# Graph rows on GpSimd, interleaved scatters and a shorter routing in the mixing part of a graph-transformer layer

## What is computed

```python
xn = layernorm(x)                                   # 6250 x 256
x = x + gnn(xn, src, dst) + mix(xn)                 # graph part and mixing part
x = x + ffn(layernorm(x))                           # two of six experts per row

# mix: k, v = instance_norm of heads of xn @ w_kv; dots = k^T v; out = (q dots / N) @ w_out + b_out
# ffn:
rh = relu(features @ router_w1 + router_b1)
expert_logits = softmax(rh @ router_w2 + router_b2)
top_w, top_i = top_k(expert_logits, 2)
routing_weights = softmax(top_w)
out = sum over the two chosen experts of routing_weight * expert(features)
```

## Time and profile before

| | us |
|---|---|
| median of 3 runs | 760.2 (759.32 to 762.78) |
| the profiled execution | 756.72 |
| its span | 754.7 |
| mixing part, first mix product to last `row_ready` | 274.3 to 413.7 |
| experts' first input transfer | from 426.8 |
| TensorE busy, share of the span | 89% |
| VectorE, ScalarE, GpSimd busy | 74%, 58%, 59% |

### The profile page before, as it was taken

One profiled execution on the slowest core, in us unless ns is written; L12 is line 12 of the kernel. 1 busy time (PEld: TensorE's weight loads), 2 busy tenths in 40 slices (PEclk: granted clock), 3 DMA queues, 4 the chain that ended last, 5 costly groups with the idle time before them and its releaser, 6 DMA issues.

```text
span 754.7 us, 15722 instructions
## 1 busy us (share of the span) xinstructions
PE 673.2 (89%) x4705; PEld 621.3 (82%) x4705; DVE 555.3 (74%) x1423; ACT 441.1 (58%) x878; POOL 448.4 (59%) x392
## 2 busy tenths in 40 slices
PE   3878999999999979889885099999999999999993
PEld 2868888888888868777764089999999999999993
DVE  5665569998888876877786357777777777777773
ACT  2546567667776636767763145665665665656651
POOL 3547388877666500325556468888888865455555
PEclk9989999999999999988995579999999999999997
DMA  8785644444444268588734478666546965654443
GB/s 223 164 191 139 162 129 127 125 127 122 128 131 129 62 211 290 170 256 249 222 99 139 130 211 191 122 126 121 113 84 100 173 114 95 98 88 58 50 44 37
DMA packets 90673, 104.68 MB, mean 139 GB/s; under 512 B 27196, under 2 KB 74746, under 8 KB 90594
## 3 DMA queue, kind: packets, MB, share of 16 engines
q1 hardware_dynamic: 58049, 70.98, 33.4%
q0 software_dynamic: 32544, 32.70, 25.0%
HBM read 53.25 MB, written 52.26 MB: 140 GB/s over the span
## 4 chain that ended last, share of the span: by engine, by line
PE 77%; DVE 10%; DMA 3%; ACT 3%; POOL 2%; issue 2%; SPq 1%; POOLq 0%; DVEq 0%; ACTq 0%
PE kv_ps L1357 10%; PE kv_ps L1358 10%; PE kv_ps L1359 10%; PE pt L1349 6%; PE d_ps L1221 6%; PE kv_ps L1198 5%; PE kv_ps L1201 5%; PE kv_ps L1199 5%; PE xt_ps L1349 3%; PE kv_ps L1298 2%; PE pt L1201 2%; PE pt L1198 2%; PE pt L1199 2%; POOL tab L588 1%; PE pt L1289 1%
## 5 line engine op out<-in xcount | busy, mean ns | idle before, releaser
L1357 PE MATMUL kv_ps<-we_h,now_h 128*128 x648 | 193.6, 299 | 3.7 <-DVE now_l L1168 2.2
L1358 PE MATMUL kv_ps<-we_l,now_h 128*128 x648 | 184.4, 285 | 0.0
L1359 PE MATMUL kv_ps<-we_h,now_l 128*128 x648 | 184.3, 284 | 0.0
L1357 PEld LDWEIGHTS kv_ps<-we_h,now_h 128*128 128x128 f32 x648 | 125.1, 193 | 5.2 <-issue 5.2
L1358 PEld LDWEIGHTS kv_ps<-we_l,now_h 128*128 128x128 f32 x648 | 125.4, 194 | 0.0
L1359 PEld LDWEIGHTS kv_ps<-we_h,now_l 128*128 128x128 f32 x648 | 124.9, 193 | 0.0
L1148 DVE TENSOR_TENSOR work<-kv_ps,be 128x256 f32<-128x256 f32 x216 | 81.7, 420 | 52.8 <-PE kv_ps L1359 52.6
L610 POOL DMA_INDIRECT out_x<-work,arena x56 | 87.6, 1564 | 41.9 <-DVE work L1156 26.0
L788 ACT ACTIVATE now_h<-pt 128x512 fp32r<-128x512 f32 x54 | 32.5, 602 | 105.9 <-PE pt L1349 105.9
L556 POOL DMA_INDIRECT alg<-al_tab,src_all x50 | 62.3, 1245 | 39.2 <-issue 25.2
L960 DVE TENSOR_REDUCE ss<-xring 125x16 f32<-125x1040 f32 x50 | 61.7, 1234 | 16.9 <-ACT xring L673 15.9
(11 more groups left out here) (249 smaller groups left out, 1836.1 us busy)
## 6 DMA issues: line engine op xcount, KB each, us to landing
arena<-tab SPq DMA_DIRECT2D x80, 131.0 KB, 2.9
xring<-in_x SPq DMA_DIRECT2D x26, 224.0 KB
xt_tab<-arena SPq DMA_DIRECT2D x10, 568.8 KB
we_h<-wt_h SPq DMA_DIRECT2D x6, 768.0 KB, 6.0
we_l<-wt_l SPq DMA_DIRECT2D x6, 768.0 KB, 8.8
weight_in<-tab SPq DMA_DIRECT2D x28, 131.0 KB, 2.6
xring<-in_x SPq DMA_DIRECT2D x5, 560.0 KB
out_x<-arena SPq DMA_DIRECT2D x12, 224.0 KB
```

The lines of the kernel that those rows point to most:

```text
L1357: pe.matmul(outp, hi[:, c, :], we_h[:, w], start=c == 0, stop=False)
L1358: pe.matmul(outp, hi[:, c, :], we_l[:, w], start=False, stop=False)
L1359: last = pe.matmul(outp, lo[:, c, :], we_h[:, w], start=False, stop=c == KC - 1)
```

## The change

- `graph_rows` moves from VectorE to GpSimd. It is one add of 125 x 512 instead of two of 125 x 256, in place: it writes into the input buffer, and `y2` is gone. `mixed_rows` reads the input buffer. GpSimd does the first three pairs ahead (`EARLY`) and then pair i+3 in its step i.
- There are seven input buffers instead of five; the two new ones lie where `y2` was. They are loaded after the experts' biases. A buffer is loaded again when `mixed_rows` has read it (`x2_done`), no longer when the graph add has (`y2_done`).
- The scatters of a group are issued two per GpSimd step, from step `ENDS[g] + 4`, each two followed by one graph add.
- Routing has 25 operations per group instead of 28 (18 linked), in three parts. The first choice is made from the logits before the exp, so it needs no division and stands in part 0 with step A; step B holds ten operations instead of sixteen; step C is as before.
- SyncE reads the start addresses of the first expert tile before it waits for the scatters.

```diff
-SLOTS = 5
+SLOTS = 7
+EARLY = 3
-AL_STEPS, R_STEPS = 6, 21
-ROUTE_STEPS = (0, 1, 9, 15)
+AL_STEPS, R_STEPS = 6, 18
+ROUTE_STEPS = (0, 4, 12)
@@ SyncE @@
-            for i in range(SLOTS):
+            for i in range(SLOTS - 2):
                 load_x2(i)
...
             for b in range(2):
                 sp.wait_ge(cv_out[b], 16 * ROUNDS)
+            for i in range(SLOTS - 2, SLOTS):
+                load_x2(i)
             for i in range(PR):
                 if i + SLOTS < PR:
-                    sp.wait_ge(y2_done, i + 1)
+                    sp.wait_ge(x2_done, i + 1)
                     load_x2(i + SLOTS)
...
             sp.wait_ge(fill_out[0], 16 * (E + 1))
+            early = [sp.value_load(tab_row[0:1, 0, h:h + 1], min_val=0, max_val=E * REG) for h in range(HB)]
             for g in range(GROUPS - RB, GROUPS):
                 sp.wait_ge(sc_out[g % RB], scattered(g))
@@ GpSimd @@
-            for g in range(GROUPS):
-                pool.wait_ge(row_ready, g + 1)
-                for j in range(2 * SIZES[g]):
-                    pool.indirect_dma_start(out=tab0, ...).then_inc(sc_out[g % RB], 16)
+            def graph_rows(i):
+                pool.wait_ge(x2_in[i % SLOTS], 32 * (i // SLOTS + 1))
+                rows = x2in[i % SLOTS].rearrange("p l (h n) -> p l h n", n=GC)
+                pool.tensor_tensor(rows, rows, gsum[:, 2 * i:2 * i + 2, :].unsqueeze(2).to_broadcast([P, 2, GH, GC]),
+                                   ALU.add).then_inc(y2_done, 1)
+            pool.wait_ge(gs_done, CHUNKS)
+            for i in range(EARLY):
+                graph_rows(i)
+            for i in range(PR + 8):
+                for g in range(GROUPS):
+                    for j in range(2 * SIZES[g]):
+                        if ENDS[g] + 4 + j // 2 == i:
+                            scatter(g, j)
+                if i + EARLY < PR:
+                    graph_rows(i + EARLY)
@@ VectorE @@
-            graph_rows(0)
...
-                dve.tensor_tensor(xr[g % RB][:, at:at + 2, 0:D], ma_ps[i % 2][0:P, :, :], y2[i % 2],
+                dve.tensor_tensor(xr[g % RB][:, at:at + 2, 0:D], ma_ps[i % 2][0:P, :, :], x2in[i % SLOTS],
                                   ALU.add).then_inc(x2_done, 1)
...
+                def first(k):
+                    link(dve.reduce_max(tws[6], lg0, axis=AX.X))
+                    return dve.tensor_tensor(oh[:, k, :, 0:m]..., lg0, bc(tws[6], EP), ALU.is_equal)
                 if part == 0:
                     dve.wait_ge(lg_done, 2 * ENDS[b])
                     link(dve.reduce_max(tws[0], lgp, axis=AX.X))
                     dve.tensor_tensor(lg1, lgp, bc(tws[0], EP), ALU.subtract).then_inc(lgx_ready, 1)
                     dve.tensor_copy(row[:, :, C_TOK].bitcast(I32), ...)
+                    dve.wait_ge(lgx_ready, b + 1)
+                    link(dve.scalar_tensor_tensor(lg0, lg1, 0.0, order, ALU.is_ge, ALU.mult))
+                    link(first(0))
                 elif part == 1:
                     dve.wait_ge(ex2_done, b + 1)
                     link(dve.reduce_sum(tws[1], lg2, axis=AX.X))
+                    link(dve.scalar_tensor_tensor(lg3, oh[:, 0]..., -4.0, lg2, ALU.mult, ALU.add))
                     link(dve.reciprocal(tws[1], tws[1]))
-                    link(dve.tensor_tensor(lg3, lg2, bc(tws[1], EP), ALU.mult))
-                    link(choose(0, lg3))
-                elif part == 2:
-                    link(dve.scalar_tensor_tensor(lg2, oh[:, 0]..., -4.0, lg3, ALU.mult, ALU.add))
-                    link(choose(1, lg2))
-                    dve.tensor_tensor(tws[4], tws[3], tws[2], ALU.subtract).then_inc(d_ready, 1)
+                    link(dve.reduce_max(tws[3], lg3, axis=AX.X))
+                    dve.scalar_tensor_tensor(tws[4], tws[3], -1.0, tws[1], ALU.add, ALU.mult).then_inc(d_ready, 1)
+                    link(dve.tensor_tensor(lg1, lg3, bc(tws[3], EP), ALU.is_equal))
+                    link(dve.tensor_tensor(lg0, lg1, order, ALU.mult))
+                    link(first(1))
                     dve.tensor_tensor_scan(cum..., carry..., oh..., 0.0, ALU.mult, ALU.add).then_inc(oh_ready, 1)
@@ loop of VectorE @@
-                if i + 1 < PR:
-                    graph_rows(i + 1)
-                for part, lag in ((3, 4), (1, 3), (2, 3), (0, 2)):
+                for part, lag in ((2, 4), (1, 3), (0, 2)):
```

43 lines of the change are left out of this document (15 added, 28 removed).

## The result

The changed kernel takes 766.2 us (763.56 to 767.05, five runs) against 760.88 us (759.32 to 762.78) for the kernel before, run beside it: ratio 1.0084, 95% interval [1.0061, 1.0107]. It is slower, by 4.6 to 8.1 us. I had predicted 756.7 us and a range up to 762.0 us. The profiled execution is one of 766.52 us, its span 764.6 us.

The account below looks back on a forecast made before the run. It took the mixing part's chain to alternate between TensorE and, in steps B and C, VectorE with ScalarE. 1.3 + 2.3 + 1.2 = 4.8 us, less 1.3 us held, gave 3.5 us: 760.2 to 756.7 us, range 751.0 to 762.0.

Parts of the forecast that it names:

- Start of the mixing part: Before the first product and first transposes: without VectorE's graph adds there, both come earlier, a gain of 1.3 us.
- Steps B and C: Routing steps: VectorE loses work, but ScalarE can give back only its waits for VectorE; a gain of 2.3 us.
- End: Between landed scatters and the first expert tile: SyncE's start addresses are read ahead, taking 1.2 us from the path.
- GpSimd, nothing on the path: Mixing loop: two scatters and a 1.1 us add make 4.1 us against a mean step of 5.1 us, costing nothing.
- The held operations: Mixing part: GpSimd's adds hold VectorE operations with two SBUF inputs; 0.25 us per group, 1.3 us lost, ends 0 and 5.5.
- The slack: VectorE, before step C's square root: slack of 0.4 us and more, said to speak against costly holds.
- slower by the held operations: Steps A to C: two held operations per group on the path, 11 us against 4.8 us gained; 766 us, chance 0.10.
- ScalarE takes all: Steps B and C give nothing, leaving start and end, 2.5 us, less some of it; 758.5 us, chance 0.25.
- GpSimd as the bound: Mixing loop: an add over 2.1 us would make GpSimd's step exceed the loop's 5.1 us; about 762 us, chance 0.03.
- the clock rival: Mixing loop: shorter TensorE idle times in step C may keep its clock up, some 5 us; 751.7 us, chance 0.17.

Follow-up runs that it names:

- f2: The changed kernel with the graph adds back on VectorE at their old place, two of 125x256; 752.73 us, ratio 0.9943 to the kernel before.
- f1: f2 with one 125 x 512 graph add per pair on VectorE, behind mix_l and in step A; 751.41 us, ratio 0.9909 to the kernel before.
- f3: The changed kernel run once more; 764.44 us, ratio 1.0078 to the kernel before.
- e1: The same kernel as f2, run on a chip with disturbed experts; 784.24 us, ratio 1.000 to the kernel before.
- e3: The changed kernel with a one-column GpSimd write and a wait before each graph add from pair 4 on; 785.03 us, ratio 0.999.
- h4: f1 with one spare-tile write on VectorE in step B of each group, ahead of line 1050's place; 764.75 us, ratio 1.0046 to the kernel before.
- g3: f1 with three chained spare-tile writes on VectorE in step B of each group; 796.01 us, ratio 1.0154 to the kernel before.
- g2: f1 with twenty extra TensorE products in step 24 and early reads ahead of the fill-up wait; 777.82 us, ratio 0.9937 to the kernel before.

## Why the prediction was wrong

**Start of the mixing part, 1.3 us.** The size was right: the first transposes come 8.6 us after G before and 8.7 in f2, 7.3 in f1. In the change they come at 8.3, and 1.0 of the gain is lost again (f3 24.4, f1 23.4 at the same clock). GpSimd does ten adds in a row there, since no scatters stand between them yet, and the sixth (282.40) runs beside line 1050 of pair 0, which takes 1.12 us instead of 0.16; ScalarE's rows and the first transposes stand behind it. I had costed the removal at this place and the holds only "in steps A to C".

The start in the changed kernel:

```profile
276.18 2.51 POOL L593 TENSOR_TENSOR xring<-xring,gsum_sb 125x512 f32<-125x512 f32 x2 [16.03 <-DVE gsum_sb L967]
...
277.05 0.39 PE L1281 MATMUL kv_ps<-bo_hl,sel_hl 128*128 128x256 f32 x1 [0.93 <-DVE wg_l L1019]
...
282.56 1.12 DVE L1050 SCALAR_TENSOR_TENSOR work<-mv,work 125x2 f32<-125x2 f32 x1
...
283.72 1.09 ACT L757 ACTIVATE staged<-work 125x256 f32<-125x256 f32 x2 [0.91 <-DVE work L1050]
```

The product starts 0.95 us after G instead of 1.57: 0.6 us earlier, where I had forecast 0.7.

**Steps B and C, 2.3 us.** Right. The way from the logits to the square root of step C is 0.5, 0.7, 0.5, 0.5 and 0.3 us shorter in f1 than before, 2.6 us in all; in f2 and e1, which keep the adds in step B, it is 2.5 and 2.8 us. That square root has no idle time before it in cycles that are not held, and the one of step B comes 0.3 us later, where I had 0.4 to 0.5.

**End, 1.2 us.** Right: R5 to the first tile is 20.6 us before, 19.3 after, 18.8 in f2, where the transfer starts 0.9 us after the last landing instead of 2.1 (I had said 0.1 to 0.3). What I missed is that the early reads stand behind the wait for the fill-up transfers, which in the change end last. The chain of waits there:

```profile
429.92 5.37 DMA tab<-skip_rows
...
435.37 0.28 SPq L482
...
436.00 0.27 SPq L482
...
437.55 2.05 DMA arena<-tab
```

**GpSimd, nothing on the path.** Right as far as waits go: the adds take 1.27 to 1.29 us where I took 1.1 and 1.29 as the upper bound, no mixed rows wait for one, and a step of GpSimd is 4.2 us (352.24 to 356.42) against 4.7 us and more of the loop.

**The held operations, 0.25 us per group.** This is the step that failed: 1.3 us in all were forecast, and moving the adds costs 11.7 us (f2 against f3). The mechanism was right and read from the right row; its price was too small by about a factor of ten in the three cycles from A1 to A4, where it delays the square root of step C by 3.2, 2.8 and 2.4 us, and it was nothing in groups 0 and 4. To these 8.5 us come 1.0 us at the start and the clock. Four things made it so:

- The length. I capped a hold at one add, "up to its own length". It begins with the scatter in front of the add, and two adds in a row make one hold: 2.7 us at 329.08. e3 shows this part.
- The number. I took a share of time in which VectorE is critical, a quarter to a third, as if the adds fell at random. They don't: `row_ready` starts the scatters and so fixes the adds against the steps A to C behind it. Both traces of the change have their long holds at the same few lines, 1050, 1068, 1082 and 1089.
- The slack. I set 0.4 us and more of slack before step C against the holds. It is there, 0.9 us, and takes up its part of each hold behind line 1050. But lines 1068 and 1050 stand ahead of it, where h4 shows none (0.57 to 0.59 us per cycle for a delay of as much), and a hold of 1.7 or 1.9 us behind line 1050 is longer than it.
- The clock. I had it as a rival on the gaining side only. With a longer wait of TensorE in step B more cycles run at 0.76 to 0.87, and such a cycle costs up to 3.4 us more. g3 shows it in its traced cycles, h4 in the clock of its runs. In the changed kernel's trace TensorE's part of the three cycles is 3.6 us longer than in f1, 2.9 of it in the cycle at 0.80; that this comes from the holds, and not from chance, that one trace can't show.

**The rivals.** The one called slower by the held operations, two per group of about 1 us on the path, 11 us against 4.8 us gained, gave 766 us with a chance of 0.10. It is what happened, 766.2 us, with 11.7 us as the price of the move. That the number fits so well is luck: it had two holds in each of five groups, and the trace has 8.5 us in three of them and the clock for the rest. I held the slack and the spacing of the adds against it; the slack is smaller than a hold and lies behind the lines that matter most, and the spacing doesn't keep the adds off them. "ScalarE takes all" is right for a part that I hadn't meant: taking the adds out of step B gave f1 nothing over f2. GpSimd as the bound was rightly low. The lower end of my range was added up wrongly: the clock rival with nothing held is 751.7 - 1.3 = 750.4 us, not 751.0; the measured time lies at the other end. A gain of 4.8 us against one loss that no row could size, in a chain whose slack I had only estimated, should have had more than 0.11 on the slower side.

## What to carry to other kernels

Before elementwise work with SBUF inputs goes to an idle GpSimd, see which small operations of VectorE on the critical chain read two inputs from SBUF: each that meets it waits to the end of the GpSimd operation, and from as early as the scatter in front of it. Where the work has to be on GpSimd, a one-column write with a wait ahead of it takes away that early part: e3 has a ratio of 0.999, where the change has 1.008 on other chips. Where VectorE has idle time anywhere in the cycle, moving the work there (here into step A and behind `mix_l`) gives the gain without the holds: 0.991 against 1.008. And price a delay in a chain that TensorE waits for at its own length plus the clock: 0.6 us in each of six cycles is 3.4 us, and the median rose by 10.9 us.

## What the runs showed of the hardware

- A VectorE operation with two SBUF inputs that starts while a scatter runs with a GpSimd add behind it, up to 0.8 us before the add starts in the records, is held to the end of the add; a one-column write with a wait in between removes that head start (longest hold 1.0 instead of 2.7 us). Two adds in a row hold as one (2.7 us). Statistics and reciprocals, with one SBUF input, were not held beside an add (32 of them). Beside a scatter alone none of 115 operations was held in the changed kernel; in f2 a copy was, once, by 0.4 us.
- A GpSimd write that reads no SBUF holds nothing, over 48 of them.
- GpSimd's in-place add of 125 x 512 with one operand broadcast takes 1.27 to 1.29 us, as long as an unbroadcast add of that size.
- The same cycle takes 19.7 us at a granted clock of 1.00 (f1) and 23.0 us at 0.78 (g2), with no held operation in either.
